# Second experts that add into the output rows slot by slot, all shared tiles ahead of them, and blocks that end without a GpSimd drain

## The reference

```python
x = x + L0_xattn(layernorm(x), ctx, ...)      # 16 heads
x = x + L0_ffn(layernorm(x))                  # 14 experts, 512 hidden, top 2
x = x + L1_xattn(layernorm(x), ctx, ...)
x = x + L1_ffn(layernorm(x))                  # below

def L1_ffn(x):                                # 2048 tokens, 8 experts, 1024 hidden, top 2
    shared = gelu(x @ Wfc_s + bfc_s) @ Wproj_s + bproj_s
    p, i = top_k(softmax(x @ Wr), 2);  p = p / p.sum(-1)
    routed = sum over the token's two experts e of  p_e * (gelu(x @ Wfc[e] + bfc[e]) @ Wproj[e] + bproj[e])
    return shared + routed
```

## Time and profile before

| what | value |
|---|---|
| median of 3 runs (lowest, highest) | 1040.72 us (1039.98, 1042.22) |
| the profiled execution's own time | 1038.13 us |
| its span, first to last instruction | 1036.3 us |
| mean granted TensorE clock | 0.963 of full speed |
| PE busy | 936.5 us, 90% of the span |
| POOL busy, DVE busy, ACT busy | 411.6, 498.2, 504.5 us |
| layer 0's experts end, `attention1` begins | 434.9, 442.9 us |
| layer 1: `shared_expert` ends, `experts` begins | 715.5, 716.3 us |
| last matmul of the span ends | 1017.9 us |

### The profile page before, as it was taken

The page is one execution under the profiler, slowest core; times in us unless marked ns, Lnnn a source line. Parts: engine busy times, 40 slices in busy tenths (PEclk is TensorE's granted clock), DMA queues, the critical chain, the costliest instruction groups (busy, mean ns, idle before and its releaser), DMA issues. The chain is left out here.

```text
span 1036.3 us, 25281 instructions
## 1 busy us (share of the span) xinstructions
PE 936.5 (90%) x7420; PEld 826.3 (80%) x7421; DVE 498.2 (48%) x2085; ACT 504.5 (49%) x1434; POOL 411.6 (40%) x534
## 2 busy tenths in 40 slices
PE   2799999788999999649999889998999999999992
PEld 2677787577899999536777679998999999999992
DVE  3587777564333343249999662222232323232315
ACT  2577777423333333238989743343343434343442
POOL 2777767200455555244555250000323333232213
PEclk9899999989899999859999989999999999999996
DMA  5966564077122222135221079200111111101107
GB/s 180 278 189 193 166 194 144 22 264 275 55 68 71 71 71 71 41 103 157 78 80 48 31 244 378 75 11 11 36 35 35 36 35 35 35 35 35 35 17 248
DMA packets 101321, 108.53 MB, mean 105 GB/s; under 512 B 9064, under 2 KB 87546, under 8 KB 100986
## 3 DMA queue, kind: packets, MB, share of 16 engines
q1 hardware_dynamic: 92272, 85.15, 25.6%
q0 software_dynamic: 8064, 22.03, 6.6%
q10 hardware_dynamic: 906, 0.37, 0.2%
HBM read 86.02 MB, written 21.50 MB: 104 GB/s over the span
## 5 line engine op out<-in xcount | busy, mean ns | idle before, releaser
L1846 PEld LDWEIGHTS experts_bank<-xT,wp 128*128 128x128 f32 x1968 | 234.8, 194 | 8.4 <-issue 4.4
L1846 PE MATMUL experts_bank<-xT,wp 128*128 128x128 f32 x1968 | 235.6, 277 | 3.7 <-DVE wp L1926 3.7
L1897 ACT ACTIVATE Hn<-experts_bank,vecT 128x128 f32<-128x128 f32 x312 | 114.3, 367 | 166.2 <-PE experts_bank L1846 147.4
L1778 POOL DMA_INDIRECT token_outputs<-yb,dst x84 | 94.7, 1127 | 215.6 <-DVE yb L1938 215.6
L1457 POOL DMA_INDIRECT rows<-token_rows,src x84 | 90.2, 1074 | 218.9 <-DVE dst L1452 119.6
L1856 PE MATMUL experts_bank<-w,Hn 128*128 x624 | 142.8, 382 | 0.0
L1938 DVE TENSOR_TENSOR yb<-experts_bank,b 128x256 f32<-128x256 f32 x84 | 35.7, 425 | 210.9 <-PE experts_bank L1856 210.9
L1926 DVE COPY wp<-w 128x1024 f32 x123 | 87.8, 714 | 94.7 <-PE experts_bank L1846 93.8
L1856 PEld LDWEIGHTS experts_bank<-w,Hn 128*128 128x128 f32 x624 | 115.4, 190 | 16.0
L1897 ACT ACTIVATE hid<-experts_bank,vecT 128x128 f32<-128x128 f32 x180 | 65.3, 367 | 103.1 <-PE experts_bank L1856 71.4
L1856 PE MATMUL experts_bank<-w,hid 128*128 x360 | 85.0, 379 | 0.0
(11 more groups left out here) (266 smaller groups left out, 1481.5 us busy)
## 6 DMA issues: line engine op xcount, KB each, us to landing
fs<-in_fside_Bx16xSxS_dram SPq DMA_DIRECT2D x32, 512.0 KB, 4.2
w<-in_L_ffn_w_dram SPq DMA_DIRECT2D x28, 512.0 KB
w<-in_L_ffn_Wfc_dram SPq DMA_DIRECT2D x8, 1024.0 KB, 13.8
w<-in_L_ffn_Wproj_dram SPq DMA_DIRECT2D x8, 1024.0 KB, 12.6
ctx<-in_ctx_dram SPq DMA_DIRECT2D x32, 128.0 KB, 4.8
token_rows<-Hn SPq DMA_DIRECT2D x32, 128.0 KB, 3.0
keys_values<-WT SPq DMA_DIRECT2D x16, 256.0 KB, 3.7
y<-token_outputs SPq DMA_DIRECT2D x16, 256.0 KB, 3.1
```

Source lines behind the costliest of these rows:

```text
L1778: pool.indirect_dma_start(out=c["yg"], out_offset=bass.IndirectOffsetOnAxis(ap=routing["dst"][:, n:n + 1].bitcast(U32), axis=0), in_=yb[n ...
L1846: last = pe.matmul(HB[f % 4][:, 0:P], piece[:, i, (f % CF) * P:(f % CF + 1) * P], xT[par][:, i], start=(i == 0), stop=(i == DC - 1))
L1897: act.activation(hid[par][:, f], HB[f % 4][:, 0:P], moe.act, bias=bias).then_inc(hid_ready, 1)
```

## The change

Layer 1 no longer writes each pair's output to a row of its own. `shared_expert` does all 16 shared tiles and stores each finished tile (x, bias and shared expert) to `out` at once. The routing matmul gets twice the columns, so that it also yields `share`, the weight of each slot's rows, and `dst` now holds the token's row itself, or a number past the end for padding, which the DMA's bounds check skips. In `experts` of layer 1, POOL first gathers, for slot n, the current sums of the slot's tokens from `out` (`get_sums(n)`), which waits until `scatter(n - 1)` has landed; DVE adds share x bias to them, then share x the matmul's result, and POOL scatters the sums back. The loads, the adds of 16 tiles and the stores behind the slots are gone, and so are the two shared tiles there. Layer 0's experts keep their way. All seven blocks are opened with `no_gpsimd_drain=True`; `end_phase` is as before. (`pad` shares a buffer with `expf`, and a semaphore `x_stored` counts the stores.)

```diff
-SHARED_FIRST = 14
...
-        block = stack.enter_context(nc.Block())
+        block = stack.enter_context(nc.Block(no_gpsimd_drain=True))
...
+def mark_slots(dve, r, n, slot_ready, w12=None):
...
+        last = dve.tensor_scalar(to[:, i, 0:S], r["first_row"][:], r["start"][:, j, b + i:b + i + 1],
                                   r["code"][:, j, b + i:b + i + 1], ALU.is_equal, ALU.mult)
+        if w12 is not None:
+            last = dve.tensor_scalar(to[:, i, S:2 * S], r["first_row"][:], r["start"][:, j, b + i:b + i + 1],
+                                     w12[:, b + i, j:j + 1], ALU.is_equal, ALU.mult)
...
-    FC, N = moe.FC, SHARED_FIRST
+    FC, N, S = moe.FC, B, moe.slots
...
             load_b2(sp, moe, weights)
+            for b in range(B):
+                sp.wait_ge(y_added, b + 1)
+                sp.dma_start(out[b], c["X"][:, b]).then_inc(c["x_stored"], 16)
...
-                    slot_rows(dve, routing, r, slots_of, inverted, made)
+                    slot_rows(dve, routing, r, slots_of[:, 0:S], inverted, made, summed=True)
+                    dve.tensor_copy(routing["share"][:], slots_of[:, S:2 * S])
...
             def scatter(n):
                 pool.wait_ge(y_ready, n + 1)
...
+                    pool.indirect_dma_start(out=token_sums, out_offset=at_rows, in_=yb[n % 2][:], in_offset=None,
+                                            bounds_check=B * P - 1, oob_is_err=False).then_inc(y_stored[n % 2], 16)
+
+            def get_sums(n):
+                if n == 0:
+                    pool.wait_ge(c["x_stored"], 16 * B)
+                else:
+                    pool.wait_ge(y_stored[(n - 1) % 2], 16 * ((n - 1) // 2) + 16)
+                pool.indirect_dma_start(out=sums[n % 2], out_offset=None, in_=token_sums, in_offset=bass.IndirectOffsetOnAxis(
+                    ap=routing["dst"][:, n:n + 1].bitcast(U32), axis=0), bounds_check=B * P - 1, oob_is_err=False
+                    ).then_inc(sums_got[n % 2], 16)
...
             for n in range(n_slots):
+                if out is not None:
+                    get_sums(n)
                 if n + AHEAD < n_slots:
                     gather(n + AHEAD)
                 scatter(n)
...
+                    share = routing["share"][:, at(n)]
+                    dve.wait_ge(sums_got[par], 16 * k + 16)
+                    dve.scalar_tensor_tensor(sums[par], b2, share, sums[par], ALU.mult, ALU.add).then_inc(biased, 1)
+                    dve.wait_ge(y_done, n + 1)
+                    dve.wait_ge(biased, n + 1)
+                    if after(n, 2):
+                        dve.wait_ge(y_stored[par], 16 * k)
+                    dve.scalar_tensor_tensor(yb[par][:], Y[par][:, 0:D], share, sums[par], ALU.mult, ALU.add
+                                             ).then_inc(y_ready, 1)
...
-            if out is not None:
-                add_tile(n_slots)
-                for b in range(4):
-                    add_routed(b)
-                add_tile(n_slots + 1)
-                for b in range(4, ON_DVE):
-                    add_routed(b)
```

More of the change, by code:

```diff
@@ L131, in build @@
         expert_w1(alloc(top), moe1, weights)
-        shared_expert(nc, sem, alloc, c, moe1, routing, weights, shared)
+        shared_expert(nc, sem, alloc, c, moe1, routing, weights, shared, out)
         end_phase()
-        experts(nc, sem, alloc, c, moe1, routing, weights, shared, out)
+        experts(nc, sem, alloc, c, moe1, routing, weights, out)
         end_phase()
@@ L1218, in table @@
         "expert": keep("expert", [P, moe.slots], I32),
+        "share": keep("share", [P, moe.slots]),
     }
@@ L1448, in slot_rows @@
     dve.wait_ge(made, 2)
-    dve.tensor_tensor(r["pad"][:], r["pad"][:], r["row"][:], ALU.add).then_inc(made, 1)
+    dve.tensor_tensor(r["pad"][:], r["pad"][:], r["late" if summed else "row"][:], ALU.add).then_inc(made, 1)
     dve.tensor_copy(routing["src"][:], r["late"][:])
@@ L1579, in _, with shared_expert @@
             slot_rows(dve, routing, r, T, inverted, made)
[L1582 to L1584 removed]
+def shared_expert(nc, sem, alloc, c, moe, routing, weights, shared, out):
+    FC, N, S = moe.FC, B, moe.slots
     w1, w2 = shared["w1"], shared["w2"]
@@ L1744, in experts @@
         if out is not None:
[L1746 to L1756, removed]
-            if out is not None:
[L1758 to L1768, removed]
+            token_sums = out.rearrange("b p d -> (b p) d")
+            sums = [c["X"][:, i] for i in two]
+            sums_got, biased = [sem(f"sums_got{i}") for i in two], sem("biased")
+        block = stack.enter_context(nc.Block(no_gpsimd_drain=True))
         @block.gpsimd
@@ L1787, in _ @@
                 scatter(n)
[L1788 to L1800 removed]
+            for i in two:
+                pool.wait_ge(y_stored[i], 16 * ((n_slots + 1 - i) // 2))
         @block.tensor
@@ L1878, in _ @@
             paired(pe, n_slots, slot)
-            for n in range(n_slots, n_all):
-                slot(n, n % 2, n // 2)
         @block.scalar
@@ L1898, in _ @@
             paired(act, n_slots, slot)
-            for n in range(n_slots, n_all):
-                act.wait_ge(y_done, n - 1)
-                for f in range(FC):
-                    act.wait_ge(hid_done, FC * n + f + 1)
-                    act.activation(hid[n % 2][:, f], HB[f % 4][:, 0:P], moe.act, bias=c["vecT1"][:, 64 + f:65 + f]
-                                   ).then_inc(hid_ready, 1)
-            if out is not None:
-                for b in range(ON_DVE, B):
-                    act.wait_ge(yt_got[b], 16)
-                    for j in two:
-                        act.activation(yt[b][:, j], yt[b][:, j], ACT.Copy, scale=routing["w12"][:, b, j:j + 1]
-                                       ).then_inc(scaled, 1)
         @block.vector
```

103 lines of the change are left out of this document (29 added, 74 removed).

## The result

The changed kernel takes 1061.18 us (median of 4 runs, 1059.89 to 1065.9) against 1040.35 us (4 runs of the kernel before on the same chip): a ratio of 1.0205, 95% interval 1.017 to 1.024. The forecast was 1023.3 us and faster; the time lies above the range too. The median is 37.9 us above the forecast. The profiled execution is the longest of the four, 1065.9 us with a span of 1064.2; it lies 4.7 us above the median.

A forecast was written before the change was run, and what follows sets the result against it. PE was taken as the bound, at 7.31 us a slot. The tail (-10.3 us) and the drains (-7.15) sum to -17.4, so 1040.7 becomes 1023.3 us; range 1018.5 to 1040.0.

The forecast's parts named there:

- the loop: Layer 1's experts, one scatter's start to the next: steps in series sum to 7.27 us, ends 6.60 and 8.84.
- the semaphore to the start of POOL's next DMA: In the slots' loop, from a scatter's landing to the start of `get_sums`: 0.28 us.
- the result to the next scatter: In the slots' loop, from the end of DVE's result step to the scatter's start: 0.28 us.
- scatter to landing: In the slots' loop, from a scatter's start until its rows have landed: 2.38 us, up to 2.77.
- `get_sums` to landing: In the slots' loop, the gather of the sums until landed: 2.7 to 3.8 us, taken as 3.0.
- DVE's two steps with sequencer: In the slots' loop, bias and result steps at 0.48 us each, plus 0.37 for DVE's sequencer (0 to 0.75).
- the 0.04 us of the forecast: Room in the second experts' slots: the loop at 7.27 us against PE's period of 7.31, so PE stays the bound.
- The drains: POOL's drain at the end of layer 0's experts: 7.25 us leave the path, 0.1 stays in `end_phase`, -7.15 us.
- rival B: At block ends, the next drain does the dropped drains' work, 0.082 us a DMA: 1039.8 us, no measurable change; chance 0.10.
- Rival C: In the loop, DVE's copies hold up POOL's descriptors, at `get_sums`: slower, 1052 us, or 1067 with slow scatters; chance 0.14.
- The tail: Program's end behind the last `down`: last two results one loop (6.97 us) apart, end at 1026.0 instead of 1036.3, -10.3 us.
- The seam and the routing: Store issue behind the moved shared tiles: +0.46 us; extra `mark_slots` hidden on DVE and wider routing matmul taken as nothing.

The follow-up runs named there:

- kernel with registers: Changed kernel with the padding check's bound in a POOL register loaded once, used by both indirect DMAs of a slot; 1024.09 us, ratio 0.983 (second sample 1020.73 us).
- early drain: Changed kernel with both bounds in a register loaded once, plus one POOL drain behind `get_sums(0)` of the second experts; 1022.61 us, ratio 0.9822.
- loop open: Changed kernel whose `get_sums` reads `token_rows` instead of the sums and doesn't wait for the scatter before it (output wrong); 1023.91 us, ratio 0.984.

## Why the prediction was wrong

**The step that failed** is the loop's "the semaphore to the start of POOL's next DMA: from the end of `yb` (855.24) to the scatter (855.52) it is 0.28", and its twin "the result to the next scatter, 0.28". Both were read from a DMA that carries its wait itself. In the diff both DMAs have a bound as a number, which no indirect DMA of the kernel before has, and the prediction didn't price that argument at all. The runs showed a register move in each place that takes the wait, and 0.78 and 0.82 us instead of 0.28. The loop by its own terms, over the two turns from 786.46 to 803.39:

| step | forecast | after | difference |
|---|---|---|---|
| scatter to landing | 2.38 | 2.93 and 2.65, mean 2.79 | +0.41 |
| landing to `get_sums` | 0.28 | 0.78 | +0.50 |
| `get_sums` to landing | 3.0 | 2.83 and 2.86 | -0.15 |
| DVE's two steps with sequencer | 1.33 | 1.23 | -0.10 |
| result to scatter | 0.28 | 0.82 | +0.54 |
| sum | 7.27 | 8.47 | +1.20 |

The two moves give 1.04 us; the scatter beside the copies gives 0.41, and in the kernel with registers, where the loop is in time again, that is gone too (2.45 in the slot at 797.59). The other two terms were too long by 0.25 together. Over 38 turns the loop is 38 x (8.37 - 7.31) = 40.3 us too long, of which 2.5 are the gap ahead of the last `get_sums`. Against the forecast's last scatter (1022.77, less the 7.15 of the drain, 1015.6) the trace has it at 1061.16, 45.5 later; the remaining 5 us are ahead of the first scatter. They lie within what executions differ by there: kernels that don't differ ahead of it start it between 737.9 and 746.4 us, and this execution was the longest of its four.

**The mechanism around the loop was right.** That the change puts a closed loop beside PE's period, that 7.31 us is the number to compare it with, and that it would fail "above all by the loop: by a landing or a sequencer step a tenth longer" held: it was a sequencer step, only half a microsecond longer and twice. The forecast thought of DVE's sequencer and bounded its share from 0 to 0.75 (0.27 measured); POOL's sequencer had one value and no upper bound.

**The size without the move was right, in part by luck.** With registers the kernel takes 1024.09, 1020.73 and, with an early drain, 1022.61 us; forecast 1023.3. The loop then has more room than the 0.04 us of the forecast: in the two slots shown the result step waits 0.32 and 0.48 us for PE, of which 0.1 stand there in the kernel after too. The gathers land in about 2.8 us instead of 3.0 (the median of 3.0 came from gathers whose issue took 1.19 us in the middle, beside a copy; that of `get_sums` takes 1.02), and DVE's steps are shorter. That PE stays the bound came out of a sum whose own ends were 6.60 and 8.84; the two errors just named helped it to the forecast's side. And in the tail two terms that its sum left out nearly cancel, as said below.

**The drains** were right: 7.26 us saved at layer 0's end (forecast 7.15), the following drains 0.145 us at most, rival B refuted. The rule behind rival B, so much a DMA, was wrong: 1.03 us behind 115 DMAs.

**Rival C** had the sign and nearly the time (1052; 1067 with slow scatters), and it named the scatter's part. But its place was wrong: in the kernel after every `get_sums` takes 1.01 to 1.03 us, none is held up. The scatter is, by 0.2 to 0.5 us, and in the changed kernel that comes with the late loop: with the loop open, moves and all, it takes 1012 ns in the median. So C's cause is an effect here. The Trainium skill (page "SBUF — State Buffer", section "SBUF: two separate sides") gives about 620 against about 3100 ns for a DMA beside a DVE copy; the runs show 1.01 against at most 1.50 us. The direction agrees, the size doesn't. The prediction gave this rule two prices, some 90 us where it cites it and 29 to 44 us where it says that rival C is the rule in full; the runs bear out neither.

**The tail** lacked the gap (3.25 us after, 1.70 with registers). Its guess that padding slots save something was right: they land after 2.13 to 2.17 us. With registers the last turn takes 7.44 us (1016.48 to 1023.92) where the forecast had 6.97, so gap and padding nearly cancel. The Trainium skill (page "DMA: Bandwidth & Descriptors", section "Anatomy of one DMA — SWDGE (gpsimd) path") fits 2.0 us plus bytes over 436 GB/s. An estimate by it is 2.0 for nothing moved and 2.3 for 128 KB; the traces have 2.15, and 2.4 to 2.9.

**The seam and the routing** were not measured by themselves. With registers the whole sum comes out within 3 us, so no run asks for a cost there.

## What to carry to other kernels

Look for what a new argument adds in front of an instruction that waits. Here a bound given as a number became an instruction of its own, it took the wait, and the DMA behind it started about 0.5 us later. Load such registers once, or ahead of the wait; the trace's MOVE in front of the DMA shows whether it worked. And when a loop through DMA is closed, price each hand-over from a row of the same form of instruction, or give it an upper bound; half a microsecond twice in each turn made 37 us between two kernels that differ in nothing else (1061.18 and 1024.09).

## What the runs showed of the hardware

- In the closed loop an indirect DMA on POOL starts 0.26 to 0.28 us after its releaser when it waits itself, and 0.76 to 0.83 us after it when a 29 ns register move in front of it waits.
- The issue of a scatter takes 1.01 us with no DVE copy beside it and 1.20 to 1.49 us when it starts 0.1 to 0.4 us behind the start of two copies, and then it ends 0.27 or 0.28 us behind the second copy. A copy that starts 1.1 us behind the scatter does nothing to it. Where the scatter started first, 0.58 us ahead of the copy, it was the copy that took longer, 0.95 instead of 0.69 us (loop open).
- With 113 indirect DMAs since the last drain, POOL stood still once for 1.4 us (2.5 us in the kernel after: 3.25 instead of 0.73), and a drain behind that took 1.03 us instead of the 7.25 behind 88. A drain among DMAs in flight took 4.6 and 4.9 us, and in both cases ended a little after the time at which they should have landed (an estimate from 2.7 to 2.8 us a gather).
- The granted clock at the start of the second experts was 1.00 in some profiled executions and 0.50 for some microseconds in others; the same 64 matmuls took 7.38 to 9.86 us.
